# Counting source nodes by one-hot matmuls: a split into 64 values and 98 quotients instead of 128 and 49

## The reference, cut to what matters

```
n = feat.shape[0]                                  # 6250
ones = jnp.ones(src.shape[0], dtype=feat.dtype)    # 206250 edges
out_deg = jnp.maximum(jax.ops.segment_sum(ones, src, num_segments=n), 1.0)
...
scale = jnp.sqrt(out_deg[src]) * jnp.sqrt(out_deg[dst])
msg = msg / scale[:, None]
```

## Time and profile before

| what | us |
|---|---|
| runs, median of 3 | 3798.14 |
| lowest and highest run | 3790.42, 3800.16 |
| profiled execution, its own time | 3788.61 |
| its span, first to last instruction | 3786.6 |
| busy: PE, DVE, POOL, ACT | 3353.8, 2751.4, 2533.2, 944.2 |
| stage of the 55 rounds, first one-hot to last matmul | 40.98 to 229.10 |

### The profile page before, as it was taken

The page is one execution under the profiler, slowest core; times in us unless marked ns, Lnnn a source line. Parts: engine busy times, 40 slices in busy tenths (PEclk is TensorE's granted clock), DMA queues, the critical chain, the costliest instruction groups (busy, mean ns, idle before and its releaser), DMA issues.

```text
span 3786.6 us, 71040 instructions
## 1 busy us (share of the span) xinstructions
PE 3353.8 (89%) x23981; PEld 2695.2 (71%) x23981; DVE 2751.4 (73%) x8573; ACT 944.2 (25%) x2408; POOL 2533.2 (67%) x2525
## 2 busy tenths in 40 slices
PE   6836999999999999688999999999999999999995
PEld 6734777877777777466777777777777777777774
DVE  8988899998989998366666666666666666666655
ACT  4041344443444443201111111111111111111111
POOL 1002777777777777377777777777777777777770
PEclk9756999999999999799999999999999999999997
DMA  5342566565565655375555555555555555555552
GB/s 146 85 159 61 154 169 164 163 165 159 162 166 162 164 159 160 112 224 141 139 138 138 144 139 139 139 137 144 139 139 138 137 143 141 137 138 144 139 125 71
DMA packets 286472, 542.02 MB, mean 143 GB/s; under 512 B 78816, under 2 KB 191728, under 8 KB 286116
## 3 DMA queue, kind: packets, MB, share of 16 engines
q0 software_dynamic: 133728, 387.52, 39.2%
q1 hardware_dynamic: 132852, 132.94, 11.9%
q10 hardware_dynamic: 19536, 17.02, 1.5%
HBM read 492.60 MB, written 44.66 MB: 142 GB/s over the span
## 4 chain that ended last, share of the span: by engine, by line
PE 30%; DVE 27%; POOL 23%; issue 11%; DMA 6%; ACT 2%; DVEq 0%; SPq 0%; POOLq 0%; ACTq 0%
POOL arena L876 21%; PE psE L1001 6%; DMA arena<-t_d,srci 4%; PE psE L1041 3%; DVE relw L1869 3%; PE psE L1258 3%; PE psE L1277 3%; PE psT L986 2%; PE psY L986 2%; DVE arena L1756 2%; PE psE L1056 2%; DVE X L2001 2%; DVE arena L1844 2%; PE psY L964 2%; DVE X L2003 2%
## 5 line engine op out<-in xcount | busy, mean ns | idle before, releaser
L876 POOL DMA_INDIRECT arena<-t_d,srci x1666 | 1586.8, 952 | 561.2 <-issue 532.5
L929 POOL DMA_INDIRECT X<-t1b_d,srci x840 | 933.8, 1112 | 596.3 <-DMA t1b_d<-arena 277.3
L1001 PE MATMUL psE<-arena 128*128 128x257 f32 x3430 | 1037.7, 384 | 52.7 <-DVE arena L1909 50.8
L1909 DVE TENSOR_TENSOR arena<-arena,psT 128x257 f32<-128x257 f32 x858 | 348.7, 420 | 382.1 <-PE psT L986 209.0
L1909 DVE TENSOR_TENSOR arena<-arena,psY 128x257 f32<-128x257 f32 x857 | 348.7, 420 | 381.7 <-PE psY L986 205.8
L1001 PEld LDWEIGHTS psE<-arena 128*128 128x128 f32 x3430 | 530.2, 190 | 109.1 <-DVE arena L1909 38.0
L1041 PE MATMUL psE<-arena,X 128*128 128x256 bf16 (+1 forms) x3675 | 532.0, 275 | 0.0
L986 PE MATMUL psT<-relw,arena 126*128 126x257 bf16 x2799 | 451.9, 274 | 16.9 <-DVE arena L1900 16.9
L986 PE MATMUL psY<-relw,arena 126*128 126x257 bf16 x2793 | 449.6, 273 | 0.0
L1056 PE MATMUL psE<-X 128*128 128x256 bf16 (+1 forms) x2520 | 403.0, 274 | 37.8 <-DMA X<-t1b_d,srci 28.8
L986 PEld LDWEIGHTS psT<-relw,arena 126*128 126x128 bf16 x2799 | 271.5, 97 | 161.6 <-DVE arena L1900 17.6
(11 more groups left out here) (356 smaller groups left out, 4333.8 us busy)
## 6 DMA issues: line engine op xcount, KB each, us to landing
arena<-types_d SPq DMA_DIRECT2D x245, 220.5 KB
arena<-t_d,srci POOLq DMA_INDIRECT x1666, 3.0
X<-t1b_d,srci POOLq DMA_INDIRECT x840
arena<-acc_d SPq DMA_DIRECT2D x98, 130.0 KB
t1b_d<-arena SPq DMA_DIRECT2D x7, 1347.5 KB, 6.4
arena<-dst_p SPq DMA_DIRECT2D x400, 1.5 KB
arena<-src_p SPq DMA_DIRECT2D x400, 1.5 KB
acc_d<-arena ACTq DMA_DIRECT2D x1, 6370.0 KB, 22.5
```

Source lines behind the costliest of these rows:

```text
L876: pool.indirect_dma_start(gath[:, n % RG, :], None, t2_d, bass.IndirectOffsetOnAxis(ap=srci[:, n:n + 1], axis=0)).then_inc(s_g[n % RG], 16)
L929: pool.indirect_dma_start(ring1[:, n % RG1, :], None, t1b_d, bass.IndirectOffsetOnAxis(ap=srci[:, at:at + 1], axis=0)).then_inc(s_g[n % RG ...
L1001: ins = nc.tensor.matmul(psE[:, b % 2, 0:DW], sel[:, n // SG % 3, k % SG, :], rows_of(n), start=False, stop=(k == C - 1))
L1909: v.tensor_tensor(rows, rows, psR[n % BANKS][:, 0:DW], ALU.mult).then_inc(s_po, 1)
```

## The change

The number is split as s mod 64 and s shifted right by 6, so that there are 64 values and 98 quotients. The one-hots of a round are 125 x 64 x 30 and 125 x 98 x 30, and the matmul of line 964 has weights 125 x 64 and a moving operand 125 x 98. The sum stands in 64 partitions and 98 columns. An even quotient holds the nodes of partitions 0 to 63 of a block, an odd one those of partitions 64 to 127. After the last round DVE clears a 64 x 128 tile `upper` (in the place of the table `counted`), copies a 64 x 64 identity into its right half, and copies the even and the odd columns of the count into `sm0` and `ssq`. PE then adds two fp32 matmuls into `psY[:, 1]`, which places the even columns in the lower and the odd ones in the upper 64 partitions, and DVE goes on from there.

```
-            v.tensor_scalar(lo_i, src_n, P - 1, None, ALU.bitwise_and)
-            link(v.tensor_scalar(hi_i, src_n, 7, None, ALU.logical_shift_right))
+            v.tensor_scalar(lo_i, src_n, LOWS - 1, None, ALU.bitwise_and)
+            link(v.tensor_scalar(hi_i, src_n, 6, None, ALU.logical_shift_right))
...
-                for one_hot, bits, wide in ((ohlo, hlo, P), (ohhi, hhi, NB)):
+                for one_hot, bits, wide in ((low_hot, hlo, LOWS), (high_hot, hhi, 2 * NB)):
...
-                    ins = nc.tensor.matmul(psY[:, 0, 0:NB], ohlo[:, n % 2, :, t], ohhi[:, n % 2, :, t],
+                    ins = nc.tensor.matmul(psY[0:LOWS, 0, 0:2 * NB], low_hot[:, n % 2, :, t], high_hot[:, n % 2, :, t],
...
+            pe.wait_ge(s_oh, EN + HN + 1)
+            nc.tensor.matmul(psY[:, 1, 0:NB], ident[0:LOWS, :], sm0[0:LOWS, :], start=True, stop=False)
+            nc.tensor.matmul(psY[:, 1, 0:NB], upper, ssq[0:LOWS, :], start=False, stop=True).then_inc(s_hmm, 1)
...
             dve.wait_ge(s_hmm, EN + HN)
-            root(degu[:, :], v.tensor_scalar(degu[:, :], psY[:, 0, 0:NB], 1.0, None, ALU.max))
+            link(v.memset(upper, 0.0))
+            v.tensor_copy(upper[:, LOWS:P], ident[0:LOWS, 0:LOWS])
+            halves = psY[0:LOWS, 0, 0:2 * NB].rearrange("p (b h) -> p h b", h=2)
+            v.tensor_copy(sm0[0:LOWS, :], halves[:, 0, :])
+            v.tensor_copy(ssq[0:LOWS, :], halves[:, 1, :]).then_inc(s_oh, 1)
+            dve.wait_ge(s_hmm, EN + HN + 1)
+            root(degu[:, :], v.tensor_scalar(degu[:, :], psY[:, 1, 0:NB], 1.0, None, ALU.max))
```

More of the change, by code:

```diff
@@ L84 @@
 LOOP = BINS * BIN
+LOWS = P // 2
 ABOVE = 1 << 13
@@ L353, in program @@
         ohlo = arena[0:NP, o:o + HG * P].bitcast(BF16).rearrange("p (r l t) -> p r l t", r=2, l=P)
+        low_hot = arena[0:NP, o:o + HG * LOWS].bitcast(BF16).rearrange("p (r l t) -> p r l t", r=2, l=LOWS)
+        high_hot = arena[0:NP, o + HG * LOWS:o + HG * LOWS + HG * 2 * NB].bitcast(BF16).rearrange(
+            "p (r l t) -> p r l t", r=2, l=2 * NB)
         o += HG * P
@@ L361, in program @@
         counted = arena[0:NP, o:o + HG * P // 2].bitcast(BF16).rearrange("p (l t) -> p l t", l=P)
+        upper = arena[0:LOWS, o:o + P]
         o += HG * P // 2
```

## The result

The changed kernel took 3902.90 us (median of 4 runs, 3897.42 to 3904.36) against 3794.28 for the kernel before (4 runs, 3788.59 to 3800.16). The ratio is 1.0287, with a 95% interval of 1.0275 to 1.0300: slower by about 109 us. The forecast was 3917 us with a range of 3842 to 3950.

What follows compares the result with a forecast made beforehand. The prediction took DVE and PE as both nearly full in the counting stage, PE becoming the bound. Stage +117.1 and join +1.9 gave +119.0 us, 3917 us counted from the 3798.1 median; range 3842 to 3950.

Steps and rivals of the forecast that it cites:

- What bounds the stage: Counting stage: DVE and PE both nearly full at 2.98 us a round; PE's 90 ns matmul pace set by its moving operand.
- The distance of the columns as the cause: Counting matmuls: moving columns 60 bytes apart each touch a new 16-byte line and pay, 1.8 ns each.
- The price per column: Counting matmuls: 5 ns fixed plus 1.743 ns a column, so 98 columns take 175.8 ns, a PE round 5.27 us.
- the prediction's own bound for 12 fixed: Counting matmuls: lower bound of the narrow range, 169 ns a matmul if 12 ns are fixed.
- The stall at round 42: After round 41 DVE is away 15.04 us for an insertion; PE waits 10.1 us for the next one-hots.
- The insertion after round 47: Shorter DVE insertion, some 4 us, fits into DVE's slack of 7.8 us and costs nothing.
- DVE's one-hots: Each round's two one-hots on DVE cost 1153 and 1686 ns, 235 ns less than before.
- The join: After the last count, copies and two fp32 matmuls add 1.9 us in all (1.4 to 2.3).
- Nothing behind the stage gives time back: Everything after the stage begins with the count, so the whole delay is carried in full: +119.0 us.
- The load of 64 columns: Weight load for the counting matmuls: 112 ns at 1.743 ns a column, hidden beside the 176 ns matmul.
- The rival in which it no longer lies beside the matmul: Counting stage: load and matmul add to 288 ns, 8.64 us a round, 4095 us in all; chance 0.06.
- The first rival: Counting stage: weight load or both reads set the pace, DVE alone bounds, -14 us, 3784 us; chance 0.10.

Runs made afterwards that it cites:

- cols49: Changed kernel with all matmuls of the stage after the first moving only 49 of the 98 columns, weights still 64 columns; 3823.69 us.
- wide128: Changed kernel with the low one-hot made 128 values wide again, so weights of 128 columns with 98 moving ones; 3909.90 us.
- movpair: Changed kernel with only the moving one-hot laid out in pairs, its columns 4 bytes apart, the weights' still 60; 3825.26 us.
- pairs: Changed kernel (64 values, 98 quotients) with both one-hots laid out in pairs, columns 4 bytes apart; 3774.81 us, 0.9960 of the kernel before.
- beforepairs: Kernel before (128 values, 49 quotients) with both one-hots laid out in pairs; 3785.68 us, 0.9986 of the kernel before.

## Why the prediction was right, point by point

- *What bounds the stage.* Right. The clock and the load were excluded from rows of before, and the runs agree: the pace is the same at both granted clocks, and `cols49`, `wide128` and `movpair` separate the load from the moving operand. The 59 ns that the prediction worked out for the load of 128 columns stand in no run by themselves; the pace before bounds them at 90.
- *The distance of the columns as the cause.* It was an inference from one pair of streams (line 964 against line 1085). It is now shown: the same 98 columns take 0.170 us at 60 bytes, 0.133 at 12 and, with the weights in pairs too, 0.046 to 0.084 at 4 bytes, by the granted clock. `movpair`, where only the moving operand changes, shows the cause by itself: 0.117 for 0.170, with the load as the new limit. The Trainium skill's rule that each access to another 16-byte line pays (SBUF — State Buffer, section Door 1: The DMA port swizzle) agrees with 20 bytes being no better than 60 and with 12 bytes lying between; it states no price.
- *The price per column.* Mis-sized. The step "I take 5 ns of the 90.4 as fixed" gave 1.743 ns a column and 175.8 a matmul; measured were 170.0, so 1.62 a column and about 11 fixed; the prediction's own bound for 12 fixed, 169, was the better choice. By this the rounds took 5.8 ns x 1650 = 9.6 us less than forecast, while the stall and the transposes (2.75 us for 2.4) took some 0.6 more and about 1 us is not broken down: the stage ended at 338.2 us instead of 346.2. The time came out 14 us under the forecast of 3917, and 1 us below the prediction's narrow range of 3904 to 3930. Of the 14, 8 are the stage's, and 3.8 come from the base: the forecast was counted from 3798.14, the median of three runs of before, which is 3794.28 with the fourth.
- *The stall at round 42.* Forecast 10.1 us, measured 10.3. The insertion after round 47 was hidden, as forecast: DVE's wait for PE and none of PE's remains there.
- *DVE's one-hots.* Forecast 1153 and 1686 ns, measured 1158 and 1683.
- *The join.* Forecast +1.9 us, measured 340.05 - 338.18 = 1.87, the two fp32 matmuls 0.66 + 0.44.
- *Nothing behind the stage gives time back.* Right: 110.9 us at the maximum and 110.9 at the write of `t_d`.
- *The load of 64 columns* was put at 112 ns and hidden. It is hidden behind 170 ns; where it sets the pace it takes 117. That 64 scattered columns are slower to load than 128 agrees with the Trainium skill (TensorE: Matmul & The Clock Gate, section Weight-path perf modes), by which the fast load wants 128 weights; whether this mode is the reason was not tried. The rival in which it no longer lies beside the matmul did not come true.
- *The first rival* (the load or a sum of reads sets the pace, 3784 us) had the right forecast for another kernel: with the columns in pairs DVE is the bound, and `pairs` lies 10.9 us below `beforepairs`, near the 235 ns a round for 55 rounds less the join's 1.9 (11.0 us).

## What to carry to other kernels

Before columns are moved from weights to the moving operand, read the pace of the matmul stream, (busy - one record) / (count - 1), at both granted clocks and against a stream of known columns: where the clock does not move it and the columns do not explain it, the layout of both operands is the next thing to try. Here either of them could set such a pace: the moving columns 0.170 us, the load of 64 scattered weight columns 0.117. In these runs a moving operand paid for each column whose distance to the next was 20 or 60 bytes, in part at 12, and not at 4. So it is worth trying an innermost index of two numbers in a one-hot tile instead of the whole batch. Here this cost DVE nothing, and a change that lost 109 us gains 15, 10.9 of them over the old split in the same layout.

## What the runs showed of the hardware that was not expected

A load of 64 weight columns was slower than one of 128 at the same distance of 60 bytes: with 49 moving columns it held the stream at 0.117 us, where the stream with 128 weight columns ran at 0.090. And a stream whose columns are scattered did not gain anything from a granted clock of 1.00 instead of 0.50, in either kernel and in `movpair`, while with both operands in pairs the same 98 columns took 0.046 us at 1.00 and 0.084 at 0.52.
